# A bias load put between two x loads on ScalarE's queue, and a split wait for the second group of four pairs

## The reference

```
w = weights[subject];  b = bias[subject]                 # 8 subjects: weights 8x64x64, bias 8x64
x = x + einsum('bct,bcd->bdt', x, w) + b[:, :, None]     # layer 0
H = einsum('btd,od->bto', x, W)                          # W 512x512
delta = (x A_k^T) B_k^T * scalings[k], k = adapter[b]    # 8 adapters of rank 16
x = x + H + delta                                        # layer 1
```

## Time and profile before

| | us |
|---|---|
| median of 3 runs | 241.74 |
| lowest, highest | 240.59, 242.06 |
| the profiled execution, as a run | 241.67 |
| its span, first to last instruction | 239.9 |
| busy: TensorE matmul / VectorE / ScalarE / GpSimd | 228.6 / 149.3 / 108.0 / 80.0 |

### The profile page before, as it was taken

One profiled execution on the slowest core, in us unless ns is written; L12 is line 12 of the kernel. 1 busy time (PEld: TensorE's weight loads), 2 busy tenths in 40 slices (PEclk: granted clock), 3 DMA queues, 4 the chain that ended last, 5 costly groups with the idle time before them and its releaser, 6 DMA issues.

```text
span 239.9 us, 9652 instructions
## 1 busy us (share of the span) xinstructions
PE 228.6 (95%) x2900; PEld 186.9 (78%) x2901; DVE 149.3 (62%) x259; ACT 108.0 (45%) x185; POOL 80.0 (33%) x277
## 2 busy tenths in 40 slices
PE   1798999999999999999999999999999999999993
PEld 1676888888888888888788888888888888888862
DVE  6798857775358735874358824875348755435753
ACT  2174573653435353563425445453426534353541
POOL 3468780710067620520046740535134141000000
PEclk9999999999999999999999999999999999999998
DMA  5956465735565474635645563655657364561333
GB/s 128 293 151 190 145 179 133 216 97 153 159 172 164 131 217 109 197 109 171 179 131 176 139 209 105 190 144 133 174 136 212 90 197 113 160 194 46 90 87 90
DMA packets 23723, 36.64 MB, mean 153 GB/s; under 512 B 6162, under 2 KB 6162, under 8 KB 23698
## 3 DMA queue, kind: packets, MB, share of 16 engines
q1 hardware_dynamic: 16640, 26.36, 40.5%
q10 hardware_dynamic: 7058, 9.97, 13.6%
HBM read 19.53 MB, written 16.78 MB: 151 GB/s over the span
## 4 chain that ended last, share of the span: by engine, by line
PE 88%; DVE 4%; DMA 2%; issue 2%; ACT 1%; ACTq 1%; POOL 0%; DVEq 0%; POOLq 0%
PE ps L901 69%; PE ps L861 14%; PE ps L837 3%; DMA x_ring<-in_x_dram 2%; DVE o_ring L558 1%; ACTq L709 1%; PE ps L793 1%; ACT x_hi L663 1%; ACT m_f L682 1%; PE ps L831 0%; DVE x_lo L538 0%; PE ps L889 0%; DVE last_parts L543 0%; PE ps L890 0%; PE ps L892 0%
## 5 line engine op out<-in xcount | busy, mean ns | idle before, releaser
L901 PE MATMUL ps<-m_hi,x_hi 128*128 x244 | 97.0, 398 | 0.0
L901 PE MATMUL ps<-m_hi,x_lo 128*128 x244 | 95.1, 390 | 0.0
L901 PE MATMUL ps<-m_lo,x_hi 128*128 x244 | 95.1, 390 | 0.0
L538 DVE TENSOR_TENSOR x_lo<-x,x_hi 128x512 fp32r<-128x512 f32 x64 | 44.4, 694 | 62.9 <-ACT x_hi L663 62.6
L374 POOL COPY p_pair<-p_all 64x64 f32 x128 | 44.6, 349 | 114.0 <-DVE x L530 96.8
L663 ACT ACTIVATE x_hi<-x 128x512 fp32r<-128x512 f32 x64 | 40.4, 632 | 55.3 <-ACT o_ring L676 30.0
L676 ACT ACTIVATE o_ring<-ps 128x512 f32<-128x512 f32 x60 | 35.9, 598 | 52.6 <-PE ps L901 51.3
L901 PEld LDWEIGHTS ps<-m_hi,x_hi 128*128 128x128 f32 x244 | 45.7, 187 | 10.7 <-issue 0.3
L901 PEld LDWEIGHTS ps<-m_hi,x_lo 128*128 128x128 f32 x244 | 45.8, 188 | 9.7
L901 PEld LDWEIGHTS ps<-m_lo,x_hi 128*128 128x128 f32 x244 | 45.8, 188 | 9.0
L530 DVE TENSOR_TENSOR x<-ps,bias_pair 128x512 f32<-128x512 f32 x64 | 43.6, 685 | 12.0 <-PE ps L861 10.8
(11 more groups left out here) (103 smaller groups left out, 79.7 us busy)
## 6 DMA issues: line engine op xcount, KB each, us to landing
x_ring<-in_x_dram SPq DMA_DIRECT2D x124, 128.0 KB, 2.7
out_dram<-o_ring ACTq DMA_DIRECT2D x64, 128.0 KB, 2.6
out_dram<-o_ring SPq DMA_DIRECT2D x64, 128.0 KB, 2.3
a_f<-in_L_cond_A_dram SPq DMA_DIRECT2D x8, 128.0 KB, 2.6
o_ring<-in_L_cond_W_dram SPq DMA_DIRECT2D x2, 256.0 KB, 4.7
o_ring<-in_L_cond_W_dram ACTq DMA_DIRECT2D x2, 256.0 KB, 6.0
x_ring<-in_x_dram ACTq DMA_DIRECT2D x4, 128.0 KB, 3.3
b_nat<-in_L_cond_Bm_dram ACTq DMA_DIRECT2D x1, 256.0 KB, 3.7
```

Of the source, the lines that this page charges most:

```text
L538: nc.vector.tensor_tensor(x1_lo[:, u % HELD], x1[:, u % 2], x1_hi[:, u % HELD], ALU.subtract).then_inc(x1_lo_ready, 1)
L901: mm = nc.tensor.matmul(ps[:, 2 + u % 2, :], part, m_tile(m, k, c), start=(c == 0 and part is hi and m is m_hi), stop=(c == TC - 1 and par ...
```

## The change

The load of the bias leaves its place behind the two parts of W and is issued by ScalarE between the upper x half of pair 0 and that of pair 1. In the third step (j = 2) TensorE waits for seven of the eight pairs' copies (`pair_ready` at 28) before the layer 0's, and for the eighth pair's (at 32) directly before the layer 0 of pair 7, the last of the four. In the steps that are written out (j = 2, 54, 58) the register load `words` now stands ahead of the waits instead of behind them.

```diff
@@ block.scalar @@
             for o in range(2, TC):
                 act.dma_start(w_nat[:, o, :], W[o * P:o * P + P, :]).then_inc(w_in[o], 16)
-            act.dma_start(bias_all[:], bias.rearrange("s d -> (s d)").rearrange("(a n) -> a n", a=1)
-                          .to_broadcast([P, S * C]).rearrange("p (s d) -> p s d", s=S)).then_inc(bias_in, 16)
...
             b = words(act, last_regs[:4], batch[0:1, 0:4], B - 1)
-            for i in range(2):
-                load_half(act, i, 1, b[2 * i + 1], x_first[i])
+            load_half(act, 0, 1, b[1], x_first[0])
+            act.dma_start(bias_all[:], bias.rearrange("s d -> (s d)").rearrange("(a n) -> a n", a=1)
+                          .to_broadcast([P, S * C]).rearrange("p (s d) -> p s d", s=S)).then_inc(bias_in, 16)
+            load_half(act, 1, 1, b[3], x_first[1])
             a_round(0, 0)
@@ quad_inputs @@
-                pe.wait_ge(pair_ready, j * 4 + 4 * L0_QUAD)
+                pe.wait_ge(pair_ready, j * 4 + 4 * (L0_QUAD - (1 if isinstance(j, int) and j == XR else 0)))
@@ step of block.tensor @@
-                if l0_pairs:
+                if l0_pairs and n is not None:
                     quad_inputs(j + 2)
...
+                if l0_pairs and n is None:
+                    quad_inputs(j + 2)
                 for i in l0_pairs:
+                    if n is None and j == 2 and i == 5:
+                        pe.wait_ge(pair_ready, 4 * (XR + L0_QUAD))
                     layer0(j + i, u + i)
```

## The result

The changed kernel takes 242.44 us (median of 13 runs, 241.78 to 244.20) against 241.27 for the kernel before beside it. The ratio is 1.0053, with a 95% interval of 1.0040 to 1.0066: 1.2 to 1.3 us slower, half a per cent, inside the 1% that I had called no change. The forecast was 241.6 by two effects that cancel. They don't cancel: the loss is clear of its interval.

What follows compares the result with a forecast made beforehand. Only delays or releases of TensorE in the first 23 us were taken to matter, both places hanging on the late bias. -0.75 and +0.72 gave -0.03 on the profiled 241.67, so 241.6 us, range 240.6 to 242.7.

Steps and rivals of the forecast that it cites:

- two effects that cancel: Third step's gain of -0.75 us and the late bias load's cost of +0.72 us, together -0.03.
- Part 1: Third step: split wait and earlier register load remove TensorE's 0.75 us of standing still, -0.75 us.
- pair 7 wait: Third step's last layer 0 waits for pair 7 apart; claimed met early, with 1.3 us to spare.
- a delay is carried to the end one for one: TensorE's first 23 us: a delay there lengthens the run equally, since TensorE's own work is the path from 22.70.
- Part 2: Bias load moved between ScalarE's x halves: it lands later and delays layer 1 of pair 0, +0.72 us.
- I take S = 11.9: GpSimd's first bias copy was put at 11.9, near the swap but 0.3 under it, costing +0.72 us.
- S: Start of GpSimd's first bias copy, 10.85 before; from 11.18 on, each us of the bias costs a us.
- the swap: Bound from above: bias and x half only change places in the queue, so S = 12.19, a loss of 1.01.
- S + 4.41: Start of layer 1 of pair 0, set by GpSimd's four pairs and pair 3's layer 0, once later than 15.59.
- The clock was put at nothing: TensorE's granted clock was read as 0.9 or more of full speed; no cost was forecast for it.
- The slower one: Bias shares its queue and DMA engines, so GpSimd waits until S = 13.3: +1.4 us, 243.0; chance 0.22.
- The faster rival: Bias load lands before 11.18, so the third step's gain stands alone: -0.75 us, 240.9; chance 0.25.

Runs made afterwards that it cites:

- register load alone: Kernel before with the register load ahead of the waits and the third step still waiting for all eight pairs: 240.72 us (0.9977).
- TensorE kept busy early: GpSimd's weights first, bias behind W, split third step, plus 12 extra small matmuls before 4.7 us: 241.33 us (1.0005).
- GpSimd's weights first: Changed kernel with GpSimd copying the weights of pairs 0 to 3 before its wait for the bias: 240.94 us (0.9987); with bias behind W, 240.69.
- idle time filled: Changed kernel plus 24 unused small matmuls between the transposes of W and layer 0 of pair 0: 242.26 us (1.0045), again 242.80 (1.0059).
- pair 0 freed: Changed kernel, but TensorE's layer 0 of pair 0 waits for the weight copies alone, VectorE's bias add for the bias copies: 242.28 us (1.0040).
- bias move alone: Kernel before with only the bias load moved between the x halves, TensorE's third step as before: 243.41 us (1.0073).
- bias ahead of x: Changed kernel with the bias load issued one wait earlier, ahead of the first x half on ScalarE's queue: 240.79 us (0.9981).

## Why the prediction was wrong

**Part 1 was right.** -0.75 forecast for the third step; -0.7 and -0.55 measured for the whole and for the register load alone, and no gap in any trace of the changed kernel. The pair 7 wait never bit. That the gap of the profiled execution (0.75) was near the mean of three that range from 0.42 to 1.25 was luck.

**That a delay is carried to the end one for one was right too.** In 16 of the 18 traces the run took 218.5 to 218.8 us more than the start of its third step. The exceptions are the run with TensorE kept busy early (219.6, its idle piece) and the first profile of before (219.0). From its third step to the group of layer 0's at 215 us that one took 0.28 us more than the first trace of the changed kernel, 0.18 of it between the groups at 78 and 92 us. This is why of the 0.71 us between the third steps of the first two profiles only 0.43 were left at 217 us.

**Part 2 failed in the step "I take S = 11.9".** S was 12.42, 12.64, 12.59 and 13.55. Two terms were too small. First, the landing. I went 0.3 under the swap, which had the bias land at 12.16; it landed at 12.20 in the first trace, almost there, and at 12.43, 12.38 and 13.34 in the others. So the swap was no upper bound. It assumed that the DMA engines stay nearly full when the loads change places, but from 8 to 12 us they moved about 90 to 190 KB less than before, which at the 240 GB/s of the earlier trace rows are, as an estimate, 0.4 to 0.8 us. Second, the hand-over. The prediction sets S at the landing plus 0.03, but in its own trace the bias landed at 3.45 + 7.2 = 10.65, 0.20 before the copy at 10.85, and in the changed kernel it is 0.22.

**The chain behind S was right in kind, a little short.** S + 4.41 was the formula for layer 1 of pair 0; the first trace had S + 4.81: 0.28 from slower GpSimd copies, 0.12 from hand-overs and the slower small matmuls. At full clock pair 3 decides and not pair 0, and with GpSimd's weights first the dependence is gone.

**The clock was put at nothing.** I read the granted clock of before as full and carried it over. The later start leaves TensorE without matmuls for 2.2 to 2.6 us in the three later traces, and it then runs at half clock for a few us. The traces with the bias in its new place and GpSimd's old order show the price, as the distance from S to the third step (the forecast had 22.65 - 11.9 = 10.75):

| trace | S | third step | distance | TensorE behind its idle time |
|---|---|---|---|---|
| changed kernel, first | 12.42 | 23.41 | 10.99 | full pace |
| idle time filled, first | 12.58 | 23.59 | 11.01 | full pace |
| idle time filled, second | 12.99 | 23.99 | 11.00 | full pace |
| pair 0 freed | 12.54 | 23.51 | 10.97 | full pace |
| changed kernel, second | 12.64 | 24.14 | 11.50 | granted 0.50 |
| changed kernel, third | 12.59 | 24.08 | 11.49 | granted 0.50 |
| changed kernel, fourth | 13.55 | 25.08 | 11.53 | granted 0.50 |
| bias move alone | 13.13 | 25.72 | 12.59 | half pace for longer, 1.00 recorded |

In these three traces the granted 0.50 added 0.5 us, whether S was 12.6 or 13.55. Over the forecast of 22.65, the second and third traces are 1.4 to 1.5 late: 0.7 from S, 0.25 from the chain, 0.5 from the clock; the fourth is 2.4 late, 1.65 of it from S. As a share of the median's loss the clock is argued, not shown, since about half of the executions have the low clock and the filler didn't lower the median. Nothing here shows why S itself varies by 1.1 us between executions.

**The rivals.** The slower one named the place, GpSimd's wait for the bias, and +1.4 for the size. The place is right. That its size is close to the measured one is in part luck: its S of 13.3 was reached in one trace of four, and in the others the longer chain and the clock, which it doesn't have, made up the rest. I gave it 0.22 because I held W's 512 KB ahead of the bias for the reason of its 7.2 us; the load then took 4.0 to 5.2 us behind one x half of 128 KB. The faster rival had nothing for it in any trace: no S in the new place lies under 12.42.

## What to carry to other kernels

Before moving a load later in a queue, find what it shares its present time with. If it fills a stretch in which the DMA engines would have less to move, "the two loads only change places" is no upper bound for its landing. Count what queues in order behind the late arrival (four pairs on GpSimd here), and let that engine do first what doesn't need it. Ask what the engine at the end of the chain does while it waits longer: here TensorE's idle time grew, and its clock fell. Look for register loads that stand behind a wait: hoisting one gave 0.55 us. The best kernels of this study are the one with the old bias place and the changed third step (240.73, ratio 0.9972), and the same with GpSimd's weights first (240.69, 0.9970); both beat the kernel before and the changed one. The register load alone (240.72, 0.9977) and the bias ahead of x (240.79, 0.9981) can't be told from them.

## What was not expected of the hardware

TensorE's pace after idle time. In the three traces in which its granted clock fell to 0.50, it had been without a matmul for 2.30, 2.21 and 2.57 us. With the bias move alone 1.82 us were followed by half pace, at a recorded clock of 1.00. In the first trace of the changed kernel (1.16 us), in the three of the kernel before (1.33, 0.96 and 1.51) and in the second with filler (1.33) it ran on at full pace. How it had run before the idle time doesn't sort these cases: the transposes of W ended at half pace both in the trace of the bias move alone and in the first one of the changed kernel.

And a float32 matmul from one partition over 512 columns took 2.00 us at that time of the program, far above what its size had led me to estimate (0.85).
